# A query and key image in DRAM: four slots per row for six, and stacks read in two transfers of 24 rows

## The reference

```python
q, k, v = ((h @ W).reshape(B, T, 16, 8) for W in (Wq, Wk, Wv))
scores = einsum("bshd,bthd->bhst", q, k) * scale      # windowed: only near keys
ctx = einsum("bhst,bthd->bshd", softmax(scores), v)
x = x + ctx.reshape(B, T, 128) @ wo
```

## Time and profile before

| | us |
|---|---|
| median of 3 runs | 2489.55 |
| lowest, highest | 2487.47, 2490.19 |
| profiled execution | 2485.17 |
| its span, first to last instruction | 2483.4 |
| busy: PE, PEld | 2090.2, 901.6 |
| busy: DVE, ACT, POOL | 1809.1, 1613.2, 520.5 |
| windowed attentions begin (projection's end) | 277.8, 663.5 |
| full attentions begin (projection's end) | 831.3, 1683.4 |

### The profile page before, as it was taken

How to read it: one execution, slowest core, us unless ns; L and a number is a source line. 1 busy time by engine, 2 the same in 40 slices (tenths; PEclk the granted TensorE clock), 3 DMA queues, 4 the chain that set the end, 5 groups by cost and what they waited for, 6 DMA issues and landing times. The chain is left out here.

```text
span 2483.4 us, 43785 instructions
## 1 busy us (share of the span) xinstructions
PE 2090.2 (84%) x15400; PEld 901.6 (36%) x15400; DVE 1809.1 (73%) x4894; ACT 1613.2 (65%) x2354; POOL 520.5 (21%) x753
## 2 busy tenths in 40 slices
PE   6497488778377799999999987848999999999696
PEld 2365255556145222222222236731222222222475
DVE  7833695442585899999999925378999999996543
ACT  3043355333244489999999963434999999999343
POOL 6176221157111000000000005720000000000075
PEclk8599699789689689999999988955999999999798
DMA  2312560211570511111011021115011011010212
GB/s 67 96 48 73 87 119 5 85 48 49 91 142 13 152 21 26 20 31 29 17 31 31 2 62 46 51 39 155 16 30 31 16 30 30 16 30 2 75 48 87
DMA packets 94743, 127.14 MB, mean 51 GB/s; under 512 B 20954, under 2 KB 72640, under 8 KB 94528
## 3 DMA queue, kind: packets, MB, share of 16 engines
q1 hardware_dynamic: 82880, 102.99, 19.0%
q0 software_dynamic: 11648, 21.36, 2.9%
HBM read 79.88 MB, written 42.40 MB: 49 GB/s over the span
## 5 line engine op out<-in xcount | busy, mean ns | idle before, releaser
L1338 ACT ACTIVATE prob<-ps 128x1024 f32<-128x1024 f32 x1024 | 989.5, 1023 | 42.4 <-PE ps L1222 22.8
L1391 DVE TENSOR_REDUCE pair_mx<-ps 128x1 f32<-128x512 f32 x1520 | 959.5, 683 | 71.1 <-PE ps L1191 69.7
L1191 PE MATMUL ps<-k_stack,q_stack 48*128 48x512 bf16 x2048 | 590.4, 402 | 27.7 <-PEq L943 8.9
L1236 PE MATMUL ps<-prob,v_head 128*32 128x512 f32 x4096 | 547.2, 606 | 1.2 <-ACT prob L1338 1.0
L1222 PE MATMUL ps<-q_stack,k_stack 51*128 51x512 bf16 x2048 | 450.3, 383 | 6.4 <-ACT prob L1338 3.8
L1191 PEld LDWEIGHTS ps<-k_stack,q_stack 48*128 48x128 bf16 x2048 | 152.7, 94 | 494.6 <-DVE pair_mx L1391 346.9
L2340 DVE TENSOR_TENSOR hid<-silu,ps 128x256 f32<-128x256 f32 (+1 forms) x190 | 87.8, 463 | 248.0 <-PE ps L2193 168.8
L1222 PEld LDWEIGHTS ps<-q_stack,k_stack 51*128 51x128 bf16 x2048 | 103.1, 93 | 302.5 <-ACT prob L1338 270.2
L1743 DVE CUSTOM_DVE_ANT_0 ps<-ps,mask 128x256 f32<-128x256 f32 (+2 forms) x512 | 179.7, 418 | 40.1 <-PE ps L1547 37.7
L1312 ACT ACTIVATE qk<-ps 128x512 f32<-128x512 f32 x264 | 157.7, 597 | 57.2 <-PE ps L1191 45.9
L2193 PE MATMUL ps<-weight_raw,block 128*128 x632 | 193.4, 429 | 0.0
(11 more groups left out here) (251 smaller groups left out, 2263.6 us busy)
## 6 DMA issues: line engine op xcount, KB each, us to landing
q_stack<-image_dram SPq DMA_DIRECT2D x88, 192.0 KB, 4.5
k_stack<-k_wide_dram SPq DMA_DIRECT2D x60, 240.0 KB, 5.2
arena<-e_rows SPq DMA_DIRECT2D x32, 256.0 KB, 4.7
k_stack<-image_dram SPq DMA_DIRECT2D x32, 192.0 KB, 4.4
image_dram<-parts SPq DMA_DIRECT2D x28, 192.0 KB, 5.4
k_wide_dram<-parts SPq DMA_DIRECT2D x2, 1800.0 KB, 17.3
image_dram<-parts SPq DMA_DIRECT2D x28, 128.0 KB, 4.9
weight_raw<-in_L_ffn_Wg_dram SPq DMA_DIRECT2D x6, 528.0 KB, 4.3
```

Of the source, the lines that this page charges most:

```text
L1191: nc.tensor.matmul(max_bank(n), rows_of(c.q_stack, b, g, ROWS, slice(t * P, (t + 1) * P)), rows_of(c.k_rows, b, g, ROWS, slice(k * CHUNK, ...
L1236: ins = nc.tensor.matmul(out, c.v_head[:, e % 2, kb, :], unit, start=(kb == 0 and e % 2 == 0), stop=(kb == TILES - 1 and e % 2 == 1), skip ...
L1338: nc.scalar.activation(c.prob[:, u % P_UNITS, :], c.ps[:, 2 * (u % 2) * CHUNK:2 * (u % 2) * CHUNK + UNIT], ACT.Exp, scale=scale).then_inc( ...
L1391: ins = nc.vector.reduce_max(mx[:, w:w + 1], max_bank(n), AX.X)
```

## The change

Slots that hold the same part twice in a row are kept once. The query image has four slots, [high, high, middle, low], and the key image [low, middle, middle, high] (the places of high and low in `parts` are swapped for keys, `HIGH` and `LOW`). A tensor is stored in two transfers, queries as slot 0 and slots 1 to 3, keys as two pairs of slots, with no repeated source. A half of a stack is read in two transfers of 24 rows, now one behind the other in partitions: the first takes slots 0 to 2 of eight columns; the second takes slots 1 to 3 of the queries, and slot 3 of the keys three times over, by a step of 0. The rows meet in the same six products, in another order. Counts follow: 8 loads per stack, 2 stores per tensor. Compute instructions keep their number and shapes.

```diff
-Q_SLOTS = (slice(0, 3), slice(3, 6, 2), slice(4, 5))
-K_SLOTS = (slice(2, 5), slice(1, 6, 4), slice(0, 1))
+KEPT = 4
+GROUPS = 2
+TERMS = SLOTS // GROUPS
+HIGH = (0, 2)
+LOW = (2, 0)
+Q_STORES = ((slice(0, 1), slice(0, 1)), (slice(1, 4), slice(0, 3)))
+K_STORES = ((slice(0, 2), slice(0, 2)), (slice(2, 4), slice(1, 3)))
+STORES = 2
...
+def load_products(engine, c, n, head, cols, rows, loaded):
+
+    image = image_of(c, n)[head * HD:(head + 1) * HD, :, cols]
+    first, last = (image[:, 0:TERMS], image[:, 1:KEPT]) if n == 0 else \
+        (image[:, 0:TERMS], image[:, KEPT - 1:KEPT].broadcast_to((HD, TERMS, cols.stop - cols.start)))
+    for group, terms in enumerate((first, last)):
+        engine.dma_start(rows[group * HD * TERMS:(group + 1) * HD * TERMS], terms).then_inc(loaded.sem, 16)
+
 def load_piece(engine, c, n, head, b, g, cols, loaded):
 
-    rows = image_of(c, n)[head * HD:(head + 1) * HD, :, cols].rearrange("d s n -> (d s) n")
     stack = (c.q_stack, c.k_rows)[n]
-    engine.dma_start(stack_rows(stack, b, g, ROWS, cols), rows).then_inc(loaded.sem, 16)
+    load_products(engine, c, n, head, cols, stack_rows(stack, b, g, ROWS, cols), loaded)
...
-    for part, where in enumerate((Q_SLOTS, K_SLOTS)[n]):
-        dst = image_of(c, n)[rows, where, cols]
-        src = c.parts[rows, n, part:part + 1, cols].broadcast_to((rows.stop - rows.start, dst.shape[1], cols.stop - cols.start))
-        sp.dma_start(dst, src).then_inc(stored.sem, 16)
+    for where, part in (Q_STORES, K_STORES)[n]:
+        sp.dma_start(image_of(c, n)[rows, where, cols], c.parts[rows, n, part, cols]).then_inc(stored.sem, 16)
...
-                nc.scalar.activation(c.parts[:, n, 0, k * CHUNK:(k + 1) * CHUNK], bank(c, u % BANKS), ACT.Identity,
+                nc.scalar.activation(c.parts[:, n, HIGH[UNITS[u][0]], k * CHUNK:(k + 1) * CHUNK], bank(c, u % BANKS), ACT.Identity,
...
-                nc.vector.tensor_tensor(c.parts[:, n, 2, cols], c.big[:, n, cols], c.parts[:, n, 1, cols], ALU.subtract)\
+                nc.vector.tensor_tensor(c.parts[:, n, LOW[UNITS[u][0]], cols], c.big[:, n, cols], c.parts[:, n, 1, cols], ALU.subtract)\
...
-    LOADS = 4
+    LOADS = 4 * GROUPS
...
-            rows = image_of(c, n)[h * HD:(h + 1) * HD].rearrange("d s n -> (d s) n")
-            engine.dma_start(rows_of(stack, b, g, ROWS, cols), rows).then_inc(stack_loaded[b].sem, 16)
+            load_products(engine, c, n, h, cols, rows_of(stack, b, g, ROWS, cols), stack_loaded[b])
...
-        c.image_dram = nc.dram_tensor("image_dram", (2, D, SLOTS, N_TOK), bf16).ap()
-        c.k_wide_dram = nc.dram_tensor("k_wide_dram", (D, SLOTS, N_TOK + CHUNK), bf16).ap()
+        c.image_dram = nc.dram_tensor("image_dram", (2, D, KEPT, N_TOK), bf16).ap()
+        c.k_wide_dram = nc.dram_tensor("k_wide_dram", (D, KEPT, N_TOK + CHUNK), bf16).ap()
```

More of the change, by code:

```diff
@@ L900, in store_parts @@
 def store_parts(c, sp, n, rows, cols, stored):
-    for part, where in enumerate((Q_SLOTS, K_SLOTS)[n]):
-        dst = image_of(c, n)[rows, where, cols]
-        src = c.parts[rows, n, part:part + 1, cols].broadcast_to((rows.stop - rows.start, dst.shape[1], cols.stop - cols.start))
-        sp.dma_start(dst, src).then_inc(stored.sem, 16)
+    for where, part in (Q_STORES, K_STORES)[n]:
+        sp.dma_start(image_of(c, n)[rows, where, cols], c.parts[rows, n, part, cols]).then_inc(stored.sem, 16)
 def first_loads(n, paired):
-    return 4 if n == 0 or n == 1 and not paired else 2
+    return 4 * GROUPS if n == 0 or n == 1 and not paired else 2 * GROUPS
 def first_stores(n, paired):
-    return 2 * PARTS if n == 1 and not paired else PARTS
+    return 2 * STORES if n == 1 and not paired else STORES
 def first_piece_of(tile):
@@ L993, in take_rest @@
                 nc.vector.scalar_tensor_tensor(c.big[:, n, cols], bank(c, u % BANKS), BIAS[n] if BIAS[n] is not None else 0.0,
-                                               c.parts[:, n, 0, cols], ALU.add, ALU.subtract).then_inc(rest.sem, 1)
+                                               c.parts[:, n, HIGH[UNITS[u][0]], cols], ALU.add, ALU.subtract).then_inc(rest.sem, 1)
             def take_low(u):
@@ L1018, in _ @@
             store_parts(c, sp, Q, rows, Q_PIECES[0], q_stored[0])
-            sp.wait_ge(*k_stored.after(2 * PARTS * 16))
+            sp.wait_ge(*k_stored.after(2 * STORES * 16))
             for g, head in enumerate(first_heads(paired)):
                 load_piece(sp, c, K, head, 0, g, WHOLE, first_loaded[0])
-            sp.wait_ge(*q_stored[0].after(PARTS * 16))
+            sp.wait_ge(*q_stored[0].after(STORES * 16))
             for g, head in enumerate(first_heads(paired)):
@@ L1035, in project_stage @@
     v_taken.passed(CHUNKS)
-    k_stored.passed(2 * PARTS * 16)
-    q_stored[0].passed(PARTS * 16)
+    k_stored.passed(2 * STORES * 16)
+    q_stored[0].passed(STORES * 16)
 def load_first_rest(c, sp, paired):
@@ L1436, in _ @@
                 store_parts(c, sp, n, slice(HD, P), (WHOLE, WIDE_KEYS)[n], stored)
-            sp.wait_ge(*stored.after(2 * PARTS * 16))
+            sp.wait_ge(*stored.after(2 * STORES * 16))
             for h in range(1, STACKS):
@@ L1452, in full_heads_stage @@
                    (st_ready, HEADS * EXP_UNITS), (exp_done, HEADS * EXP_UNITS), (pv_done, HEADS * TILES), (out_taken, PAIRS), (inverted, PAIRS),
-                   (stored, 2 * PARTS * 16)):
+                   (stored, 2 * STORES * 16)):
         sig.passed(n)
@@ L1626, in load_half @@
         for n, stack in enumerate((c.q_stack, c.k_stack)):
-            rows = c.image_dram[n, head * HD:(head + 1) * HD].rearrange("d s n -> (d s) n")
-            engine.dma_start(rows_of(stack, b, g, ROWS, slice(0, N_TOK)), rows).then_inc(stack_loaded[b].sem, 16)
+            load_products(engine, c, n, head, WHOLE, rows_of(stack, b, g, ROWS, WHOLE), stack_loaded[b])
     def store_shift(engine, e, g):
@@ L1799, in load_stacks @@
             def load_stacks(h):
-                sp.wait_ge(*stored[h % 2].after((h + 1) // 2 * 2 * PARTS * 16))
+                sp.wait_ge(*stored[h % 2].after((h + 1) // 2 * 2 * STORES * 16))
                 if h >= PAIR_STACKS:
@@ L1828, in window_heads_stage @@
     for b in range(2):
-        stored[b].passed((PAIRS // 2 - (1 - b)) * 2 * PARTS * 16)
+        stored[b].passed((PAIRS // 2 - (1 - b)) * 2 * STORES * 16)
     for b in range(PAIR_STACKS):
```

## The result

The changed kernel takes 2500.71 us (median of 5 runs, 2499.19 to 2503.61); the kernel before took 2490.19 in the runs beside it (2487.47 to 2495.77). The ratio is 1.0046, 95% interval [1.0034, 1.0057]: 10.5 us slower, where 10.6 us faster was forecast. The profiled execution took 2500.50 us (before: 2485.17).

The account below looks back on a forecast made before the run. 26.5 us were taken to hang on late stack transfers in the attention stages, behind stores bound by bytes. Terms -3.7 and -2.9 (windowed) and -4.0 (full) sum to -10.6 us: 2489.55 to 2479.0 us, range 2471 to 2487.

Parts of the forecast that it names:

- SyncE's issue: SyncE's queue: 0.46 us per 16- or 48-row transfer, 0.34 per 8-row one; added loads and fewer stores balance in the projection.
- The queries' rest: Windowed stages, loads of pair 0's remaining queries ahead of pair 1's stores: four become eight, +0.9 us per stage.
- Pair 1's eight issues: Windowed stages: costed at nothing, since SyncE is free some 3 us before the stores land; without that cover 1.9 us.
- issue sets the end: Rival: SyncE reaches pair 1's loads only as stores land, 1.9 us per windowed stage, pair 2 by 0.5; 2483 us, chance 0.15.
- The stores: Four slots for six, bound by bytes: pairs 1 and 2 -4.9 and -4.6 us (windowed stages), full stages -8.3 us.
- The engines: Loads from 8-row sources use half the engines: share about 0.5, 175 GB/s, +0.1 us per 192 KB, +0.3 per pair.
- The rival worked out beside it: Half the engines, half the rate: the loads of pairs 1, 2 and 3 land later, +9.7 us, 2499 us; chance 0.10.
- Who is late next: Windowed stages: pair 2 waits 0 and +0.3 us more, the shift rows +0.2 in the second stage.
- The 12 us that later pairs were said to load ahead: Windowed stages: pairs after pair 2 load some 12 us or more ahead.
- the full stages: Head 1's stacks arrive earlier, covering both TensorE waits, so VectorE's idle 2.36 and 1.60 us go: -4.0 us.

Follow-up runs that it names:

- eight_engines: The kernel before with an unused seventh image slot, so each 48-row load no longer merges into one run and uses half the engines: 2508.97 us, ratio 1.0070.
- two_queues: The changed kernel with ScalarE issuing half 1 of the loads for pair 0's remaining queries and pair 1 in the windowed stages: 2491.12 us, ratio 1.0008.
- order_only: The kernel before with SyncE issuing pair 1's loads ahead of pair 2's stores in the windowed stages: 2490.60 us, ratio 1.0004.
- order_late_store: The kernel before with pair 1's loads ahead of pair 2's stores, and pair e+3's stores behind shift rows and pair e+2's loads: 2482.78 us, ratio 0.9967.

## Why the prediction was wrong

- **The step that failed is SyncE's issue.** It priced a 24-row load at 0.34 to 0.46 us, from stores of 8 rows and loads of 48; it takes 0.69. Going from four to eight loads in the projection was put at +1.4 to +1.8 and balanced by fewer stores to 0; the loads cost about four times 0.92 us more, and the stages start 3.30, 2.29, 1.95 and 1.90 us later. The queries' rest, put at +0.9, takes 5.55 us for 2.52. Pair 1's eight issues were put at nothing, under a cover of 3 us in which the stores were still to land: the first goes out at 295.31 and the last is done at 302.06, while the last store (issued at 293.97) lands 5.1 us later, at 299.1, so that 3 us of issue stand open. The rival "issue sets the end" had this mechanism, with 0.46 us an issue, and so came to 2483.
- **The row that was nearest was in the forecast.** All transfers from which the price was taken have the same outer rows on both sides (48 to 48, 16 x 3 to 16 x 3). The only transfer of SyncE there whose two sides differ in shape, the shift rows (three rows of 16 blocks from 48 rows), stands in the earlier trace rows with 0.74 us. It was read for its time of issue, not for its price.
- **TensorE's clock was not in the sum.** The new waits cost their length and, by the matched stretches above, some 3.6 us more at the lower clock. The forecast said that TensorE keeps every instruction, and priced none of them anew.
- **The stores: right, if a little too small.** Pairs 1 and 2 take 10.7 us from the first issue to the last landing (288.34 to 299.1) for 16.5 before (280.39, and 5.1 us behind the issue at 291.79): -5.8 for -4.9. In the first full stage they take 16.5 us (855.97 to 872.5) for the 16.6 of the forecast, but begin 8.6 us after the stage for 2.9 before, +5.7 instead of +2.0 to +2.8.
- **The engines: right.** The loads' share is 0.46 (about 0.5 forecast), and half the engines move 177 GB/s where a whole transfer is issued at once. The Trainium skill, "DMA: Bandwidth & Descriptors", section "Rules for kernel authors", speaks against an outermost dimension under 16. The share of 0.46, and 177 GB/s for 195 in eight_engines, agree with its direction; the 140 GB/s of the change don't bear on it, since they are the pace of the issues. The rival worked out beside it had 2499 us, near the 2500.7 measured, but that is a coincidence: 96 KB were to take 1.03 us and take 0.69, and what two_queues got back was issue. What busy engines wait for, which was argued against this rival, no run shows.
- **Who is late next: too small.** Pair 2 waits 2.30 us in the second stage, with 0.3 more than before forecast, and the shift rows 2.04 and 1.64, with 0.2 forecast. For the loads of pairs 2 and 3, now sixteen issues of 0.69 us, the queue needs 11 us (309.96 to 321.0) for what took 3.7 (306.31 to 310.03), and the next shift rows stand behind that. The 12 us that later pairs were said to load ahead hold for the first stage only: in the second, pair 3's last load landed at 702.2, 6.9 us before its use, and even so no new wait came before pair 3. In the full stages, where -4.0 was forecast, 3.7 us were won before head 1 and 3.9 lost at the start.
- What the runs leave open: how much half the engines would cost at the old price of issue. No cut tried has both, so the 19 us of eight_engines are not divided between the two.

## What to carry to other kernels

A queue's issues are work with a price per transfer and per pattern; before splitting a transfer, look for a row of the same pattern on both sides, and if there is none, leave the price open upwards. Fewer bytes written do not help a reader that stands behind more issues in the same queue. When a late transfer is moved ahead, follow what it now stands in front of and what falls behind it: order_only won 5 us and lost them to the shift rows, order_late_store kept them. And when a split adds waits, read the granted clock behind them too.

## What was not expected of the hardware

Issue times of SyncE by pattern, one transfer each: 48 rows in one run 0.46 us, 24 in one run 0.41, 32 in one run 0.48; 8 x 6, 8 x 3 and 8 x 2 rows from a source that isn't one run 0.69 to 0.72, at 1 KB rows as at 4 KB. ScalarE takes 0.71 and 0.73 us for the same 24-row loads (issued at 284.00, 284.71 and 285.44 in two_queues), so the price belongs to the pattern and not to SyncE.

TensorE's granted clock fell from 1.00 to a mean of 0.60 of full speed behind an idle time of 2.04 us that the change had brought, and the 28 matmuls there took 1.93 us for 1.08. A wait can cost more than its length.
